# Two-layer attention kernel: the maxima of the second layer reduced one 512-column block at a time in a ring of three PSUM banks

## The chip, the cores and the metric

One core of a Trainium2 chip runs the whole program. The metric is the device time of one launch in microseconds; lower is better. One profiled execution of the kernel before was recorded, and all rows below come from it.

## The reference, cut to what matters

The input `x` has 4 batches of 1024 tokens and 128 features. A first attention layer with 8 heads of 64 is followed by a "graph" of six nodes, each a full attention over the tokens of its batch with 8 heads of 16. Only the graph is touched by the change.

```
for c in range(NUM_NOD):                       # 6 nodes
    q = ew[c, 0] * (nodes[in_q] @ We[eq] + be[eq])
    k = ew[c, 1] * (nodes[in_k] @ We[ek] + be[ek])
    v = ew[c, 2] * (nodes[in_v] @ We[ev] + be[ev])
    o = _mha(q, k, v, Wq[c], Wk[c], Wv[c], Wo[c])   # softmax over 1024 keys
    nodes[c] = act_w[c] * o + q
```

The softmax needs, for every query row and head, the maximum over the 1024 keys of the scores, before any exponential of that head can be taken.

## The kernel before

Six nodes times four batches make 24 **units**, and the graph works through them one after the other. Everything in a unit stands in a fixed order that Python loops write out for each engine; there is no scheduler. Engines meet through semaphores alone.

**Rounds.** TensorE (PE) walks through 74 rounds in a full unit. 64 of them are score rounds: two matmuls of 50x512 fill two banks of PSUM (`ps_max`, two buffers of 1024 columns used in turn), and ScalarE (ACT) takes the exponential of all 1024 columns in one instruction into `pt_b`. The other ten are listed in `PLAN`: round 2 and 50 turn maxima (`turn`, line 1563), 8 and 24 make the output of the unit before (`output`, lines 1611 and 1612), 11, 14, 17 and 20 project queries and keys of two units ahead (`project`, line 1524), 30 and 34 make values (`values`, line 1532). `bank_free` lets a round start only when the round two before it has been read out of the same `ps_max` buffer.

**Contexts.** After every second score round PE multiplies four exponentials with the values (`contexts`, line 1603, 4 matmuls that appear as 8 records, output `ps_ctx`). A unit has 32 such groups. This text calls the stretch from the start of one group to the start of the next a **step**, and names a step by the round that ends it: step 44 holds the group that begins after round 42, and rounds 43 and 44. Steps with nothing but score rounds and maxima are called plain; there are 22 in a unit (1, 6, 23, 28, 33, then every second number from 38 to 48 and from 53 to 73), and ten mixed ones: 4 and 51 with a turn, 9 and 26 with an output, 12, 15, 18 and 21 with a projection, 31 and 36 with values.

**Maxima.** While a unit runs, PE also makes the raw scores of the **next** unit, 128 blocks of 128 queries by 512 keys (48x512 matmuls, line 1556), only to find their row maxima. They go to three banks of PSUM: `ps_pair` (two banks) and `ps_misc` (one). VectorE (DVE) reduces what is there to maxima (`tensor_reduce`, line 1777). A piece is two blocks in `ps_pair` for even numbers and one block in `ps_misc` for odd numbers (`SIZES`), so there are 86 pieces. PE may fill a piece when DVE has reduced the piece two before it, the last user of the same banks:

```
if w > 1 or p >= 2:
    pe.wait_ge(mx_done, NM * (w - 1) + p - 1)
```

Heads lie in pairs on rows 0 to 47 and 64 to 111 of the array; two matmuls in a row on different halves overlap, and `in_turn` orders the two of a pair for that.

**The table.** `PIECE_SLOT` says where each piece stands. Slot 2r is just ahead of round r's own matmuls, slot 2r+1 just behind them and ahead of a context group. DVE takes the pieces in the same order. The table holds for units with all ten other rounds or as many rounds in all (the first 22); unit 22, with fewer rounds, spreads its pieces evenly, and the last unit has none.

Between pieces DVE takes four short reciprocals per unit, and at the end of each half of the pieces a small maximum over two chunks of keys (`mx_final`, line 1785), for which the turns wait.

Of the kernel before, what the change touches and what calls it, by code (L numbers as in the profile page):

```python
# [25 lines left out]
ALU = mybir.AluOpType  # L26
AX = mybir.AxisListType

P = 128
BATCH, TOK, DIM = 4, 1024, 128  # L30
HEADS, QUAD, DV = 8, 4, 16
SLOT = 32
CHUNK = 512
NCHUNK = TOK // CHUNK
KB = TOK // P
# [20 lines left out]
MROW_B = DV * len(TERMS)  # L56
# [13 lines left out]
BLOCKS = 2 * PIECES  # L70
# [1186 lines left out]
def graph(nc, psM, psP, psO, psX, sid, wpd, wvd, wfd, node, partd, invd, stored, units, x1d, ln_g, ln_b, out_rows):  # L1257
# [3 lines left out]
    with ExitStack() as ctx:  # L1261
# [71 lines left out]
        ROUND = [rounds_of(u) for u in range(UNITS)]  # L1333
        BASE = [sum(len(ROUND[w]) for w in range(u)) for u in range(UNITS + 1)]

        SIZES = []
        for q in range(2):
            while sum(SIZES) < BLOCKS * (q + 1):
                SIZES.append(min(2 - len(SIZES) % 2, BLOCKS * (q + 1) - sum(SIZES)))
        NM = len(SIZES)  # L1340
        HALF_M = NM // 2

        def exps(u, n):
            return NS // 2 * u + (n + 1) // 2
# [5 lines left out]
        def steps_at(u, r):  # L1350
# [4 lines left out]
        GROUP_ROUND = {BASE[u] + r: (S + 1) // KB - 1 for u in range(UNITS) for r in range(len(ROUND[u]))  # L1355
                       for S in steps_at(u, r) if S % KB == KB - 1}

        PIECE_SLOT = (2, 2, 4, 6, 9, 10, 12, 14, 16, 19, 19, 21, 24, 25, 26, 27, 29, 31, 32, 33, 35, 37,
# [3 lines left out]
        SLOTS_INNER = 2 * (NS // 2 + len(PLAN))  # L1362

        def pieces_at(u, r, half):
# [12 lines left out]
        with nc.Block() as block:  # L1377
# [141 lines left out]
            def _(pe):  # L1519
# [16 lines left out]
                last_rows = [None]  # L1536
# [9 lines left out]
                def maxima(w, p):  # L1546

                    if p % HALF_M == 0:
                        pe.wait_ge(stacked[p // HALF_M], STACK * (w + 1))
                    if w > 1 or p >= 2:  # L1550
                        pe.wait_ge(mx_done, NM * (w - 1) + p - 1)
                    at = sum(SIZES[:p])
                    for k in in_turn([(at + k) % 2 for k in range(SIZES[p])]):
                        pair, qb, kc, odd = (at + k) // (BLOCKS // 2), (at + k) // 4 % KB, (at + k) // 2 % 2, (at + k) % 2
                        rows = slice(P // 2 * odd, P // 2 * odd + MROW_B)
                        ins = pe.matmul((psP, psX)[p % 2][:, CHUNK * k:CHUNK * k + CHUNK],  # L1556
                                        qs[w % 2][rows, pair, P * qb:P * qb + P],
                                        ks[w % 2][rows, pair, CHUNK * kc:CHUNK * kc + CHUNK], start=True, stop=True)
                    ins.then_inc(mx_ready, 1)

                def turn_maxima(w, q, to):
                    pe.wait_ge(mx_final, 2 * w + q + 1)
# [210 lines left out]
            def _(dve):  # L1773
                def maxima(w, p):
                    dve.wait_ge(mx_ready, NM * (w - 1) + p + 1)
                    at, n = sum(SIZES[:p]), SIZES[p]
                    nc.vector.tensor_reduce(mx2[:, at:at + n], (psP, psX)[p % 2][:, 0:CHUNK * n].rearrange("p (h n) -> p h n", h=n),  # L1777
                                            AX.X, ALU.max).then_inc(mx_done, 1)
                    if p % HALF_M == HALF_M - 1:
                        q = p // HALF_M  # L1780
                        dve.wait_ge(mx_done, NM * (w - 1) + p + 1)
                        if w:
                            dve.wait_ge(mt_ready, 2 * (w - 1) + q + 1)
                        both = mx2[:, BLOCKS * q:BLOCKS * q + BLOCKS].rearrange("p (n k h) -> p n k h", k=2, h=2)
                        nc.vector.tensor_tensor(mx[:, PIECES * q:PIECES * q + PIECES].rearrange("p (h n) -> p n h", h=2),
                                                both[:, :, 0], both[:, :, 1], ALU.max).then_inc(mx_final, 1)
# [201 lines left out]
```

## Time and profile before

| | |
|---|---|
| time, median of 3 runs | 3016.4 us (3011.99 to 3019.83) |
| time of the profiled execution | 3020.31 us |
| its span, first to last instruction | 3018.5 us |
| busy share of the span | PE 95%, DVE 79%, ACT 72%, GpSimd 12% |
| mean granted clock of TensorE | 0.977 |

Busy time of PE is made of modelled ends of overlapping matmuls, so 95% doesn't say that the array is full. What a piece costs is read from the starts of instructions in the timeline: the start of the next one, less the start of this.

### The profile page before, as it was taken

Reading aid. Unit: us, or ns where it says so; the run is one execution under the profiler, and the core shown is the slowest. Engines: PE = TensorE matmul, PEld = TensorE weight load, DVE = VectorE, ACT = ScalarE, POOL = GpSimd, SP = SyncE. Lnnn points to the kernel's source line nnn. Section 1 sums busy time; section 2 is a strip of 40 time slices with the busy share of each in tenths; the row PEclk is TensorE's granted clock in tenths of the full one; section 3 lists DMA queues with packets and bytes.
Section 4 is the critical chain, followed back from the end, with each engine's and each line's share of the span. In section 5 each row is a group of like instructions: output and inputs, shape, how many; then the busy total and the mean of one; then the engine's idle time right before and its main releaser. Section 6 shows DMA issues by size and latency. Waiting matters only on the chain. (4 is left out here: it accounts for less than half of the span.)

```text
span 3018.5 us, 49064 instructions
## 1 busy us (share of the span) xinstructions
PE 2854.5 (95%) x18975; PEld 1291.1 (43%) x18975; DVE 2385.2 (79%) x3019; ACT 2159.6 (72%) x2738; POOL 353.0 (12%) x314
## 2 busy tenths in 40 slices
PE   6899999998699999999999999999999999999986
PEld 5556656654333333333333333333333333333332
DVE  7656566665778888888888888888888888888865
ACT  3556555555368888878787878787878788878776
POOL 0000000000001111111111111110111110111100
PEclk8999999999789999999999999999999999999998
DMA  7000000013423544453544453544454544444302
GB/s 160 25 9 16 16 12 12 5 62 72 93 60 97 114 80 98 88 116 96 117 78 100 88 114 100 113 78 103 93 107 102 111 77 105 95 102 105 66 21 67
DMA packets 146190, 239.49 MB, mean 79 GB/s; under 512 B 56802, under 2 KB 97142, under 8 KB 142630
## 3 DMA queue, kind: packets, MB, share of 16 engines
q1 hardware_dynamic: 145958, 236.36, 35.5%
q8 instruction: 150, 2.46, 0.4%
q14 instruction: 82, 0.67, 0.1%
HBM read 162.53 MB, written 70.98 MB: 77 GB/s over the span
## 5 line engine op out<-in xcount | busy, mean ns | idle before, releaser
L1749 ACT ACTIVATE pt_b<-ps_max 128x1024 f32<-128x1024 f32 x1516 | 1489.0, 1023 | 296.3 <-PE ps_max L1568 291.6
L1777 DVE TENSOR_REDUCE mx_b<-ps_pair 128x2 f32<-128x1024 f32 (+1 forms) x989 | 1191.5, 1205 | 110.5 <-PE ps_pair L1556 99.3
L1603 PE MATMUL ps_ctx<-pt_b,vs 128*32 128x512 f32 x6144 | 823.7, 608 | 1.8 <-ACT c_b L1732 1.8
L1777 DVE TENSOR_REDUCE mx_b<-ps_misc 128x1 f32<-128x512 f32 x989 | 676.4, 684 | 164.5 <-PE ps_misc L1556 160.8
L1568 PE MATMUL ps_max<-qs,ks 50*128 50x512 f32 x3032 | 766.4, 434 | 4.1 <-ACT pt_b L1749 0.6
L1556 PE MATMUL ps_pair<-ks,qs 48*128 48x512 f32 x1955 | 525.8, 464 | 24.3 <-DVE mx_b L1777 22.4
L1556 PE MATMUL ps_misc<-ks,qs 48*128 48x512 f32 x989 | 447.6, 453 | 12.1 <-DVE mx_b L1777 7.3
L1568 PEld LDWEIGHTS ps_max<-qs,ks 50*128 50x128 f32 x3032 | 346.6, 186 | 225.6 <-ACT pt_b L1749 137.6
L1556 PEld LDWEIGHTS ps_pair<-ks,qs 48*128 48x128 f32 x1955 | 202.7, 184 | 381.1 <-DVE mx_b L1777 350.9
L1556 PEld LDWEIGHTS ps_misc<-ks,qs 48*128 48x128 f32 x989 | 182.7, 185 | 380.5 <-DVE mx_b L1777 291.9
L931 ACT ACTIVATE pt<-ps_max,cb 128x512 f32<-128x512 f32 x340 | 214.6, 685 | 180.9 <-PE ps_max L658 117.6
L994 DVE TENSOR_REDUCE mx<-ps_max 128x2 f32<-128x1024 f32 x172 | 206.6, 1220 | 62.9 <-PE ps_max L629 39.2
L1603 PEld LDWEIGHTS ps_ctx<-pt_b,vs 128*32 128x32 f32 x6144 | 121.4, 108 | 239.3 <-issue 228.5
L651 PE MATMUL ps_max<-qs,ks 64*128 64x512 f32 x1020 | 162.9, 424 | 20.8 <-ACT pt L931 14.0
L931 ACT ACTIVATE pt<-ps_pair,cb 128x512 f32<-128x512 f32 x172 | 108.8, 684 | 93.9 <-PE ps_pair L658 53.8
L1928 POOL TENSOR_TENSOR part<-full,part 128x512 fp32r<-128x512 f32 x88 | 112.6, 1280 | 382.9 <-ACT part L1700 382.9
L1940 POOL TENSOR_TENSOR cn_b<-c_b,rec_b 128x512 f32<-128x512 f32 x48 | 62.0, 1292 | 702.1 <-DMA rec_b<-invd 668.5
L720 PE MATMUL ps_ctx<-pt,vs 128*32 128x512 f32 x1024 | 136.7, 607 | 0.6 <-ACT c_a L907 0.6
L651 PEld LDWEIGHTS ps_max<-qs,ks 64*128 64x128 f32 x1020 | 84.1, 186 | 114.2 <-issue 48.6
L994 DVE TENSOR_REDUCE mx<-ps_pair 128x2 f32<-128x1024 f32 x84 | 102.5, 1220 | 30.4 <-PE ps_pair L629 17.0
L1943 POOL TENSOR_TENSOR cn_b<-c_b,rec_b 128x512 f32<-128x512 f32 x47 | 60.3, 1284 | 415.1 <-DMA rec_b<-invd 401.0
L651 PE MATMUL ps_pair<-qs,ks 64*128 64x512 f32 x516 | 82.0, 423 | 9.1 <-ACT pt L931 6.9
(225 smaller groups left out, 2178.7 us busy)
## 6 DMA issues: line engine op xcount, KB each, us to landing
partd<-part SPq DMA_DIRECT2D x22, 2048.0 KB, 9.5
qs<-partd SPq DMA_DIRECT2D x288, 128.0 KB, 5.6
ks<-partd SPq DMA_DIRECT2D x288, 128.0 KB, 6.7
xv<-node SPq DMA_DIRECT2D x26, 512.0 KB, 5.5
xf<-node SPq DMA_DIRECT2D x24, 512.0 KB, 4.7
xq<-node SPq DMA_DIRECT2D x23, 512.0 KB, 3.8
xk<-node SPq DMA_DIRECT2D x23, 512.0 KB, 4.8
rec_b<-invd SPq DMA_DIRECT2D x368, 32.0 KB, 1.8
```

The costliest lines, as they stand in the source:

```text
L651: ins = pe.matmul(to[:, CHUNK * odd:CHUNK * odd + CHUNK], minus[rows] if a is None else a[q][rows, j, keys], b[q][rows, j, queries], start ...
L720: ins = pe.matmul(psO[SLOT * i:SLOT * i + SLOT, :], vs[q][:, kb, i], pt[:, s % 2, i], start=kb == 0, stop=kb == KB - 1)
L931: ins = act.activation(pt[:, s % 2, 2 * j + odd], slot("score", hh, n)[:, CHUNK * odd:CHUNK * odd + CHUNK], ACT.Exp, scale=SCALE_A, bias=c ...
L994: nc.vector.tensor_reduce(out, slot("maxima", hh, p)[:].rearrange("p (k n) -> p k n", k=2), AX.X, ALU.max).then_inc(mx_done, 1)
L1556: ins = pe.matmul((psP, psX)[p % 2][:, CHUNK * k:CHUNK * k + CHUNK], qs[w % 2][rows, pair, P * qb:P * qb + P], ks[w % 2][rows, pair, CHUNK ...
L1568: return pe.matmul(to[:, CHUNK * (n % 2):CHUNK * (n % 2) + CHUNK], ks[u % 2][rows, h // 2, P * kb:P * kb + P], qs[u % 2][rows, h // 2, CHU ...
L1603: ins = pe.matmul(psO[SLOT * i:SLOT * i + SLOT, :], vs[u % 2][:, kb, QUAD * (s // HALF_STEPS) + i], pt[:, (QUAD * S + i) % ENTRIES], start ...
L1749: act.activation(pt[:, e:e + 2].rearrange("p k n -> p (k n)"), at[:], ACT.Exp, scale=SCALE_B).then_inc(exp_done, 1)
L1777: nc.vector.tensor_reduce(mx2[:, at:at + n], (psP, psX)[p % 2][:, 0:CHUNK * n].rearrange("p (h n) -> p h n", h=n), AX.X, ALU.max).then_inc ...
L1928: nc.gpsimd.tensor_tensor(part[:, qk, 1, cols], full[:, qk, cols], part[:, qk, 0, cols].bitcast(F32), ALU.subtract).then_inc(split_done, 1)
L1940: nc.gpsimd.tensor_tensor(cn[:, 0, c], c32[:, c], rec[0][:], ALU.mult).then_inc(cn_done, 1)
L1943: nc.gpsimd.tensor_tensor(cn[:, 1, c], c32[:, c], rec[1][:], ALU.mult).then_inc(cn_alone, 1)
```

## The change

The maxima of the graph's units are made and reduced one block a piece: 128 pieces of 512 columns instead of 86 of 1024 and 512. The three banks become a ring of single banks, in the order first half of `ps_pair`, `ps_misc`, second half of `ps_pair`. PE may fill a piece when the piece three before it has been reduced. The table has 128 entries from slot 0 to 147.

```
-        SIZES = []
-        for q in range(2):
-            while sum(SIZES) < BLOCKS * (q + 1):
-                SIZES.append(min(2 - len(SIZES) % 2, BLOCKS * (q + 1) - sum(SIZES)))
-        NM = len(SIZES)
-        HALF_M = NM // 2
+        NM = 2 * BLOCKS
+        HALF_M = BLOCKS
+        MAX_SLOTS = (psP[:, 0:CHUNK], psX[:], psP[:, CHUNK:TOK])
+
+        def max_slot(w, p):
+            return MAX_SLOTS[(NM * (w - 1) + p) % 3]
...
-        PIECE_SLOT = (2, 2, 4, 6, 9, 10, 12, 14, 16, 19, 19, 21, 24, 25, 26, 27, 29, 31, 32, 33, 35, 37,
+        PIECE_SLOT = (0, 1, 3, 4, 6, 6, 8, 9, 10, 12, 12, 14, 16, 16, 17, 17, 19, 20, 21, 21, 23, 25,
...
-                    if w > 1 or p >= 2:
-                        pe.wait_ge(mx_done, NM * (w - 1) + p - 1)
-                    at = sum(SIZES[:p])
-                    for k in in_turn([(at + k) % 2 for k in range(SIZES[p])]):
-                        pair, qb, kc, odd = (at + k) // (BLOCKS // 2), (at + k) // 4 % KB, (at + k) // 2 % 2, (at + k) % 2
-                        rows = slice(P // 2 * odd, P // 2 * odd + MROW_B)
-                        ins = pe.matmul((psP, psX)[p % 2][:, CHUNK * k:CHUNK * k + CHUNK],
-                                        qs[w % 2][rows, pair, P * qb:P * qb + P],
-                                        ks[w % 2][rows, pair, CHUNK * kc:CHUNK * kc + CHUNK], start=True, stop=True)
-                    ins.then_inc(mx_ready, 1)
+                    if w > 1 or p >= 3:
+                        pe.wait_ge(mx_done, NM * (w - 1) + p - 2)
+                    pair, qb, kc, odd = p // (BLOCKS // 2), p // 4 % KB, p // 2 % 2, p % 2
+                    rows = slice(P // 2 * odd, P // 2 * odd + MROW_B)
+                    last_rows[0] = odd
+                    pe.matmul(max_slot(w, p), qs[w % 2][rows, pair, P * qb:P * qb + P],
+                              ks[w % 2][rows, pair, CHUNK * kc:CHUNK * kc + CHUNK], start=True, stop=True).then_inc(mx_ready, 1)
...
-                    at, n = sum(SIZES[:p]), SIZES[p]
-                    nc.vector.tensor_reduce(mx2[:, at:at + n], (psP, psX)[p % 2][:, 0:CHUNK * n].rearrange("p (h n) -> p h n", h=n),
-                                            AX.X, ALU.max).then_inc(mx_done, 1)
+                    nc.vector.tensor_reduce(mx2[:, p:p + 1], max_slot(w, p), AX.X, ALU.max).then_inc(mx_done, 1)
```

How PE's rows stand in three steps of a full unit follows; `ps_pair` and `ps_misc` are maxima (x2 is two blocks), `ps_max<-qs,ks` are scores, `ps_ctx` the context group that begins a step and the one that begins the next. Line numbers of the changed kernel differ by a few.

Step 42, plain. Before:

```order
L1603 MATMUL ps_ctx<-pt_b,vs 32x512 x4
L1568 MATMUL ps_max<-qs,ks 128x512 x2
L1556 MATMUL ps_misc<-ks,qs 128x512
L1556 MATMUL ps_pair<-ks,qs 128x512 x2
L1568 MATMUL ps_max<-qs,ks 128x512 x2
L1603 MATMUL ps_ctx<-pt_b,vs 32x512 x4
```

Now:

```order
L1602 MATMUL ps_ctx<-pt_b,vs 32x512 x4
L1557 MATMUL ps_misc<-ks,qs 128x512
L1557 MATMUL ps_pair<-ks,qs 128x512
L1567 MATMUL ps_max<-qs,ks 128x512 x2
L1557 MATMUL ps_pair<-ks,qs 128x512
L1567 MATMUL ps_max<-qs,ks 128x512 x2
L1557 MATMUL ps_misc<-ks,qs 128x512
L1602 MATMUL ps_ctx<-pt_b,vs 32x512 x4
```

The step held three blocks between its two score rounds; it now holds four, two at its beginning, one in the middle and one at its end.

Step 26, with the output of the unit before (`xf,wf` and `cn_b,wf`). Before:

```order
L1603 MATMUL ps_ctx<-pt_b,vs 32x512 x4
L1556 MATMUL ps_pair<-ks,qs 128x512 x2
L1611 MATMUL ps_max<-xf,wf 128x512
L1612 MATMUL ps_max<-cn_b,wf 128x512
L1556 MATMUL ps_misc<-ks,qs 128x512
L1556 MATMUL ps_pair<-ks,qs 128x512 x2
L1568 MATMUL ps_max<-qs,ks 128x512 x4
L1556 MATMUL ps_misc<-ks,qs 128x512
L1603 MATMUL ps_ctx<-pt_b,vs 32x512 x4
```

Now:

```order
L1602 MATMUL ps_ctx<-pt_b,vs 32x512 x4
L1557 MATMUL ps_pair<-ks,qs 128x512
L1557 MATMUL ps_misc<-ks,qs 128x512
L1610 MATMUL ps_max<-xf,wf 128x512
L1611 MATMUL ps_max<-cn_b,wf 128x512
L1557 MATMUL ps_pair<-ks,qs 128x512 x2
L1567 MATMUL ps_max<-qs,ks 128x512 x2
L1557 MATMUL ps_misc<-ks,qs 128x512
L1567 MATMUL ps_max<-qs,ks 128x512 x2
L1602 MATMUL ps_ctx<-pt_b,vs 32x512 x4
```

Six blocks have become five: behind the output stood four, the last of them just ahead of the contexts, and now stand three.

Step 36, with values (`wv_b,xv`). Before:

```order
L1603 MATMUL ps_ctx<-pt_b,vs 32x512 x4
L1556 MATMUL ps_pair<-ks,qs 128x512 x2
L1532 MATMUL ps_max<-wv_b,xv 128x128 x4
L1556 MATMUL ps_misc<-ks,qs 128x512
L1556 MATMUL ps_pair<-ks,qs 128x512
L1568 MATMUL ps_max<-qs,ks 128x512 x2
L1556 MATMUL ps_misc<-ks,qs 128x512
L1568 MATMUL ps_max<-qs,ks 128x512 x2
L1556 MATMUL ps_pair<-ks,qs 128x512 x2
L1603 MATMUL ps_ctx<-pt_b,vs 32x512 x4
```

Now:

```order
L1602 MATMUL ps_ctx<-pt_b,vs 32x512 x4
L1557 MATMUL ps_misc<-ks,qs 128x512
L1557 MATMUL ps_pair<-ks,qs 128x512
L1534 MATMUL ps_max<-wv_b,xv 128x128 x4
L1557 MATMUL ps_pair<-ks,qs 128x512
L1557 MATMUL ps_misc<-ks,qs 128x512
L1567 MATMUL ps_max<-qs,ks 128x512 x2
L1557 MATMUL ps_pair<-ks,qs 128x512
L1567 MATMUL ps_max<-qs,ks 128x512 x2
L1557 MATMUL ps_pair<-ks,qs 128x512
L1602 MATMUL ps_ctx<-pt_b,vs 32x512 x4
```

Of the seven blocks six are left; the last place held a piece of two and holds one block.

Over a unit of the table, the blocks per step were and are:

| steps | blocks before | blocks now |
|---|---|---|
| plain: 55, 71 | 4 each | 4 each |
| plain: 59 | 5 | 4 |
| plain: 42, 44, 61, 73 | 3 each | 4 each |
| plain: 33 | 3 | 2 |
| the other 14 plain | 3 each | 3 each |
| turn: 4, 51 | 5, 6 | 5, 6 |
| output: 9, 26 | 6, 6 | 6, 5 |
| projection: 12, 15, 18, 21 | 4, 6, 6, 6 | 5, 6, 6, 5 |
| values: 31, 36 | 6, 7 | 6, 6 |

## Rows read from the trace of the kernel before

**Rows 1.** The page, busy time of each engine over the span.

```profile
PE 2854.5 (95%) x18975; PEld 1291.1 (43%) x18975; DVE 2385.2 (79%) x3019; ACT 2159.6 (72%) x2738; POOL 353.0 (12%) x314
```

**Rows 2.** One line's instructions: turns, with count, first and last start.

```profile
L1563 PE MATMUL ps_max<-ident_sb,mx_b x43: 283/284/287, 926.6 to 2822.1; 128*32 128x128 f32 x43
```

**Rows 3.** Windows: one unit: length, busy PE, PEld, DVE, ACT, POOL, clock, DMA.

```profile
1466.53:1556.66 90.13, 88.78 (x549) 34.84 (x547) 78.62 (x93) 72.63 (x87) 13.67 (x13) 1.00 0.47 99
```

**Rows 4.** Groups on DVE in that unit: busy us, mean ns, idle before.

```profile
L1777 DVE TENSOR_REDUCE mx_b<-ps_pair 128x2 f32<-128x1024 f32 x43 | 52.3, 1217 | 4.6 <-PE ps_pair L1556 4.1
L1777 DVE TENSOR_REDUCE mx_b<-ps_misc 128x1 f32<-128x512 f32 x43 | 29.4, 684 | 7.1 <-PE ps_misc L1556 7.0
```

**Rows 5.** Timeline of a plain step with three blocks: start, length, instruction.

```profile
1520.71 1.07 PE L1603 MATMUL ps_ctx<-pt_b,vs 128*32 128x512 f32 x8
...
1522.84 1.07 PE L1603 MATMUL ps_ctx<-pt_b,vs 128*32 128x512 f32 x8
```

**Rows 6.** Timeline of a plain step with four blocks.

```profile
1530.92 1.06 PE L1603 MATMUL ps_ctx<-pt_b,vs 128*32 128x512 f32 x8
1531.91 0.50 PE L1556 MATMUL ps_misc<-ks,qs 48*128 48x512 f32 x1
...
1532.45 0.69 DVE L1777 TENSOR_REDUCE mx_b<-ps_misc 128x1 f32<-128x512 f32 x1 [0.29 <-PE ps_misc L1556]
...
1533.20 0.50 PE L1556 MATMUL ps_misc<-ks,qs 48*128 48x512 f32 x1
1533.63 0.64 PE L1603 MATMUL ps_ctx<-pt_b,vs 128*32 128x512 f32 x4
```

**Rows 7.** Timeline of a plain step with five blocks.

```profile
1535.77 1.07 PE L1603 MATMUL ps_ctx<-pt_b,vs 128*32 128x512 f32 x8
...
1537.31 1.22 DVE L1777 TENSOR_REDUCE mx_b<-ps_pair 128x2 f32<-128x1024 f32 x1 [0.32 <-PE ps_pair L1556]
...
1538.59 0.50 PE L1556 MATMUL ps_pair<-ks,qs 48*128 48x512 f32 x2 [0.63 <-DVE mx_b L1777]
1539.02 0.64 PE L1603 MATMUL ps_ctx<-pt_b,vs 128*32 128x512 f32 x4
```

**Rows 8.** Timeline of step 26, with the output.

```profile
1494.14 1.06 PE L1603 MATMUL ps_ctx<-pt_b,vs 128*32 128x512 f32 x8
...
1497.48 0.49 PE L1556 MATMUL ps_misc<-ks,qs 48*128 48x512 f32 x1
...
1497.59 0.69 ACT L1726 ACTIVATE nt_b<-ps_max,wf 128x512 f32<-128x512 f32 x1 [1.60 <-PE ps_max L1612]
...
1498.76 0.50 PE L1556 MATMUL ps_misc<-ks,qs 48*128 48x512 f32 x1
1499.19 0.64 PE L1603 MATMUL ps_ctx<-pt_b,vs 128*32 128x512 f32 x4
```

**Rows 9.** Timeline of step 36, with values.

```profile
1507.33 1.06 PE L1603 MATMUL ps_ctx<-pt_b,vs 128*32 128x512 f32 x8
...
1510.38 0.69 DVE L1777 TENSOR_REDUCE mx_b<-ps_misc 128x1 f32<-128x512 f32 x1 [0.29 <-PE ps_misc L1556]
...
1510.99 0.68 DVE L1777 TENSOR_REDUCE mx_b<-ps_pair 128x1 f32<-128x512 f32 x1
...
1511.73 0.50 PE L1556 MATMUL ps_pair<-ks,qs 48*128 48x512 f32 x2
...
1512.16 1.06 PE L1603 MATMUL ps_ctx<-pt_b,vs 128*32 128x512 f32 x8
```

**Rows 10.** Timeline: behind a projection, pair, scores, single, then contexts.

```profile
1483.26 0.50 PE L1556 MATMUL ps_pair<-ks,qs 48*128 48x512 f32 x2
1483.60 0.40 PE L1568 MATMUL ps_max<-qs,ks 50*128 50x512 f32 x2
1483.84 0.40 PE L1556 MATMUL ps_misc<-ks,qs 48*128 48x512 f32 x1
1484.16 0.64 PE L1603 MATMUL ps_ctx<-pt_b,vs 128*32 128x512 f32 x4
```

8 rows, old and new, of the table PIECE_SLOT are left out of this document.

## The prediction, made before the changed kernel was run

> **What bounds the kernel now.** I read the page first: over the span PE is busy 95%, DVE 79%, ACT 72% [rows 1]. PE's figure is made of modelled ends, so it says where to look and not how full PE is. Then one line's instructions: 43 turns, two a unit, from 926.6 to 2822.1 us, which makes 21 units of (2822.1 - 926.6) / 21 = 90.26 us each [rows 2]. The kernel is thus a period repeated some 22 times, and the change is worth 22 times what it does to one. In the windows the unit from 1466.53 to 1556.66 is 90.13 us long at full clock (1.00, the level of 2.4 GHz), DVE busy 78.62 us of it and ACT 72.63 [rows 3]. No engine but PE is near its end on the average, so the unit's length is PE's own work plus what PE stands still for. The grouping of DVE shows where the slack lies: 4.6 us and 7.1 us of idle time, all of it waiting for blocks that PE had not yet made [rows 4]. PE and DVE wait for each other in turn, and the timeline of single steps tells how.
>
> A context group holds PE 0.99 us (1530.92 to 1531.91) [rows 6]. A plain step with three blocks is 1522.84 - 1520.71 = 2.13 us [rows 5]. With four blocks it is 1533.63 - 1530.92 = 2.71 [rows 6], with five 1539.02 - 1535.77 = 3.25 [rows 7]. Counting step by step in the whole stretch from 1466 us on, and in unit 22 at the end, whose steps stand in another order, the same lengths come back: 2.12 to 2.20 for three blocks, 2.69 to 2.71 for four (eight steps, of which one stands in the rows), 3.25 to 3.26 for five (six steps). So a block beyond three costs (3.25 - 2.13) / 2 = 0.56 us, though two matmuls on different halves together take only 1483.84 - 1483.60 = 0.24 us [rows 10]. The extra is a wait, and rows 6 show its links. The first block of the step starts at 1531.91, DVE starts on it 0.54 us later (1532.45), runs 0.69, and 0.06 us after its end (1533.14) the fourth block starts, at 1533.20, in the same bank; contexts follow 0.43 us behind. The fourth block can't come sooner than 1.29 us after the first, and a step that begins and ends with a block, four in all, is 0.99 + 1.29 + 0.43 = 2.71 us. With a piece of two in the last place it waits for the first pair: 1537.31 + 1.22 + 0.06 = 1538.59, as the row has it, and the step is 3.25 [rows 7].
>
> **The change, part by part.** *The ring.* Before, a pair waits for the pair two pieces back and a single for the single two back: always the same bank, which means three blocks back. Now it is written as three pieces back, and it is three blocks back again. What falls away is that a block waits for its neighbour in a pair: the pair's banks come free at start + 1.28, a single's at start + 0.75, both from the rows above. Only where a pair was waited for does this help: step 59 and step 36. A four-block step already waits for a single, and the chain of 1.29 us stands in it unchanged.
>
> *DVE's work.* Next to each other on DVE, a single starts 0.61 us after a single (1510.38 to 1510.99) [rows 9], although each is 0.69 long. A pair is 1217 ns against 684 for a single [rows 4]; with the same overlap of 0.08 it holds DVE 1.14. A unit costs 43 x (1.14 + 0.61) = 75.3 us before and 128 x 0.61 = 78.1 now: 2.8 us more of DVE in a unit in which it idles 11.7 [rows 4]. In a three-block step it has 2.13 - 3 x 0.61 = 0.30 us left. So this part costs nothing as long as that cover holds; without it, 2.8 us a unit. The Trainium skill (Perfetto Trace Analysis, section Optimizing Scalar/DVE Operations) speaks against the change here: it gives DVE some 125 ns of overhead for each instruction on PSUM and advises to group when the engine is saturated. By that figure 42 more instructions would be an estimated 5.3 us; the trace's pitch says 2.8.
>
> *The table.* This is the larger part, since a block's price depends on the step it falls in. Over the 22 plain steps, the excess over three blocks was 1 + 1 + 2 = 4 and is now seven steps with one each: 3 x 0.565 = **+1.70 us** a unit. Step 33 drops to two blocks, an even run of six matmuls that begins and ends two by two; 0.12 less, between 0 and 0.24: **-0.12**.
>
> Step 26 is 1499.19 - 1494.14 = 5.05 us, its last block at 1498.76 waiting for the first behind the output (1497.48 + 1.28) [rows 8]. With that block gone the next lock is ACT: it copies the output until 1497.59 + 0.69 = 1498.28, which is 0.80 us after the output's end, and the last two scores go into that buffer. They start at about 1498.35 and contexts 0.38 behind, 1498.73 instead of 1499.19: **-0.45**.
>
> Step 36 is 1512.16 - 1507.33 = 4.83 [rows 9]. Its last pair waited until 1511.73 at the end of a chain of two reductions. The first block behind the values stood at 1510.38 - 0.54 = 1509.84, 2.51 us into the step. Now the last block waits for this one, so the step is 2.51 + 1.29 + 0.43 = 4.23: **-0.60**.
>
> Step 21 loses one block of six. Matmuls on the two halves go by pairs: 0.34, 0.24, and 0.32 for a last single, 0.90 for five [rows 10]; a run of four is between 0.58 and 0.90. I take **-0.27**. Step 12 gains a block by the same rule at 0 to 0.23; I take 0, since it makes a run of three into one of four. In steps 4 and 51 the last block now waits for a single that stands a reduction later in DVE's queue: about **+0.16** in all, at most 0.4.
>
> The sum is 1.70 - 0.12 - 0.45 - 0.60 - 0.27 + 0.16 = +0.42 us a unit. In the steps with a projection, third and fifth blocks come to their bank within 0.1 us of its release (the third of a chain is free at 0.53 + 2 x 0.61 + 0.75 = 2.50 us after the first started, PE wants it at 2.5). For these I add 0.15, between 0 and 0.5. Then 22 x (0.42 + 0.15) = **+12.5 us**. Made against the profiled execution, 3020.31, that is 3033; its own time stands 3.9 us above the median of the runs shown, so for a median I say 3016.4 + 12.5 = **3029**. Unit 22 keeps its excess (16 blocks beyond three in its plain steps before and now), and the last unit has no pieces. What is queued behind a waiting block on PE is the score, and behind that ACT; ACT idles 17 us of the unit [rows 3] and follows PE's step.
>
> **The rivals.** *The finer ring frees PE (faster).* The fourth block of a step finds its bank free, because DVE begins on single blocks as they come. Were a four-block step to cost as little as one of three, seven steps would save 7 x 0.565 = 3.95 us and the unit be 0.57 - 3.95 = -3.4 us, 2942 us in all. The Trainium skill (Perfetto Trace Analysis, section Optimizing Scalar/DVE Operations) has a sentence for this side: if Scalar or Vector aren't saturated but cause bubbles on other engines, breaking up instructions may let work complete sooner. Against it stands that the waited-for block is already a single in rows 6 and the link is no shorter. A half of it, by waits in the mixed steps that go fully (0.3 each in ten steps, 3 us a unit), gives 0.57 - 3 = -2.4 us and 2963. It decides by one number: with seven four-block steps, each 0.08 us cheaper, the sum is zero, which is a first-to-fourth distance of 1.2 us instead of 1.29. I give the faster side 0.24, most of it near 3000, where the mixed steps gain more than I took.
>
> *DVE becomes the bound (slower).* If single reductions followed at 0.68 instead of 0.61, DVE would need 128 x 0.68 = 87 us and two for the rest in a unit of 90; the chains of three in the six projection and value steps come 0.14 late each, some 0.8 us, and the four-block steps find DVE still busy at their first block. I price it at 1.5 us a unit more: 3029 + 33 = 3062. The pitch of rows 9 speaks against it; 0.12.
>
> *Nothing is left of it.* The table's loss and the mixed steps' gain cancel to 0.2 us a unit: 3012 to 3021. Both are near 2 us, so an error of a fifth does it; 0.24.
>
> **How the numbers follow.** My forecast, 3020 to 3042 by the bounds of its terms (0.2 to 1.2 us a unit), has 0.4. A measurement of this kernel can tell about 0.3%, 9 us, from no change; part of the forecast lies inside. Slower by over 0.3%: most of my own case and the DVE case, 0.46; within: 0.30; faster: 0.24. The range must hold eight in ten: up to the middle of the DVE case, 3055, and down into the faster one, 2988.
>
> **What would show it.** In the profile after: a unit of 90.7 us between turns; plain four-block steps at 2.7 us with a first-to-fourth start distance of 1.29; DVE busy 80 to 84 us of it, with singles 0.61 apart where they queue; steps 26 and 36 near 4.6 and 4.2. I am wrong if four-block steps are short, if singles stand further apart than 0.61, or if two blocks in neighbouring banks disturb each other.

## The result, and the profile after

The changed kernel takes 3034.4 us in the median of 4 runs (3032.61 to 3036.22); the kernel before took 3015.5 beside it. The ratio is 1.0058, interval 1.0039 to 1.0077: slower by 11.8 to 23 us. Below, the medians of two experiments leave out one slow execution each (3447 and 3761 us, at granted clocks of 0.74 and 0.66). The profiled execution took 3035.97 us with a span of 3034.1. First the page of the changed kernel, busy time over the span:

```profile
PE 2891.3 (95%) x18975; PEld 1297.1 (43%) x18975; DVE 2446.9 (81%) x3985; ACT 2171.3 (72%) x2738; POOL 352.8 (12%) x314
```

These are to be held against [rows 1]: DVE has 966 instructions and 61.7 us more, PE as many matmuls as before and 36.8 us more of modelled time. A matmul that is issued less tightly counts as longer, so this figure can't say where PE stood still. The turns give the period, as in [rows 2] (one line's instructions, with first and last start):

```profile
L1562 PE MATMUL ps_max<-ident_sb,mx_b x43: 284/285/285, 930.5 to 2836.7; 128*32 128x128 f32 x43
```

That is (2836.7 - 930.5) / 21 = 90.77 us a unit against 90.26, 10.7 us over 21 units. Of the 15.6 us between the two spans, 3.9 lie ahead of the first of these turns (930.5 against 926.6) and 1.0 behind the last. The windows of one unit in the middle of the graph (length, busy PE, PEld, DVE, ACT, POOL, clock, DMA):

```profile
1473.70:1564.37 90.67, 89.86 (x547) 34.79 (x547) 81.58 (x135) 73.09 (x87) 13.61 (x13) 1.00 0.47 99
```

Against [rows 3] the unit is 0.54 us longer at the same clock (medians over all units: 90.74 and 90.15), and DVE works 2.96 us more in it. The groups of DVE in that unit (busy us, mean ns, idle before):

```profile
L1775 DVE TENSOR_REDUCE mx_b<-ps_pair 128x1 f32<-128x512 f32 x86 | 56.2, 682 | 5.2 <-PE ps_pair L1557 4.5 <-PE ps_misc L1557 0.2
L1775 DVE TENSOR_REDUCE mx_b<-ps_misc 128x1 f32<-128x512 f32 x42 | 28.6, 681 | 3.8 <-PE ps_pair L1557 2.2 <-PE ps_misc L1557 1.3
L1782 DVE TENSOR_TENSOR mx_b<-mx_b 128x32 f32<-128x32 f32 x3 | 2.1, 706 | 0.1
```

DVE still waits for PE for 9.0 us, where it waited 11.7 [rows 4]. The third row is the small maximum over two chunks of keys; its three instructions in this stretch take 706 ns in the mean.

Step 44, one of the four that grew from three blocks to four, in the timeline (start, length, instruction):

```profile
1525.08 1.06 PE L1602 MATMUL ps_ctx<-pt_b,vs 128*32 128x512 f32 x8
1526.08 0.50 PE L1557 MATMUL ps_misc<-ks,qs 48*128 48x512 f32 x1
...
1526.61 0.69 DVE L1775 TENSOR_REDUCE mx_b<-ps_misc 128x1 f32<-128x512 f32 x1 [0.23 <-PE ps_misc L1557]
...
1527.36 0.50 PE L1557 MATMUL ps_misc<-ks,qs 48*128 48x512 f32 x1
1527.78 0.64 PE L1602 MATMUL ps_ctx<-pt_b,vs 128*32 128x512 f32 x4
```

The chain of [rows 6] is unchanged: the first block at 1526.08, its reduction from 1526.61 to 1527.30, the fourth block in the same bank 0.06 later, 1.28 us after the first, contexts 0.42 behind. The step is 2.70. Step 36 ends now as follows, to be held against [rows 9]:

```profile
1513.89 1.06 PE L1602 MATMUL ps_ctx<-pt_b,vs 128*32 128x512 f32 x8
...
1515.42 0.69 DVE L1775 TENSOR_REDUCE mx_b<-ps_pair 128x1 f32<-128x512 f32 x1 [0.37 <-PE ps_pair L1557]
1516.03 0.68 DVE L1775 TENSOR_REDUCE mx_b<-ps_misc 128x1 f32<-128x512 f32 x1
1516.40 0.49 PE L1557 MATMUL ps_pair<-ks,qs 48*128 48x512 f32 x2
...
1517.68 0.50 PE L1557 MATMUL ps_pair<-ks,qs 48*128 48x512 f32 x1
1518.11 0.64 PE L1602 MATMUL ps_ctx<-pt_b,vs 128*32 128x512 f32 x4
```

The first block behind the values starts 2.51 us into the step, the last one 1.28 later, and the step is 4.22. Singles on DVE stand 0.61 apart (1515.42, 1516.03).

Read off in this way, from one context group to the next, the steps compare so (us). Each column shows the same unit, the eighth, of its kernel; four kernels of the experiments below stand beside the two, and "last version" is the one with two blocks moved. The 9 steps left out, of three or six blocks, are within 0.05 us of before in all of these. The last row is the median length of a unit over the whole graph.

| step | before | after | ring, old places | old pairs, new places | three-block table | last version |
|---|---|---|---|---|---|---|
| 4 | 3.26 | 3.57 | 3.30 | 3.47 | 3.34 | 3.34 |
| 12 | 3.63 | 3.71 | 3.63 | 3.67 | 4.00 | 4.00 |
| 15, 18 | 3.90, 3.89 | 3.89, 3.91 | 3.95, 3.96 | 3.85, 4.14 | 3.90, 3.97 | 3.92, 3.95 |
| 21, 23 | 3.91, 2.18 | 3.60, 2.13 | 3.98, 2.24 | 4.08, 2.14 | 4.13, 2.13 | 3.61, 2.12 |
| 26 | 5.05 | 4.61 | 5.05 | 4.63 | 4.96 | 4.63 |
| 33 | 2.12 | 1.90 | 2.13 | 1.90 | 2.12 | 2.12 |
| 36 | 4.83 | 4.22 | 4.81 | 5.07 | 4.42 | 4.22 |
| 38, 40 | 2.13, 2.17 | 2.13, 2.13 | 2.12, 2.25 | 2.12, 2.13 | 2.25, 2.13 | 2.12, 2.14 |
| 42, 44 | 2.13, 2.12 | 2.71, 2.70 | 2.13, 2.14 | 2.71, 2.13 | 2.25, 2.14 | 2.23, 2.69 |
| 46, 51 | 2.13, 3.84 | 2.12, 3.90 | 2.13, 3.89 | 2.19, 4.12 | 2.41, 3.91 | 2.15, 3.91 |
| 55, 71 | 2.71, 2.70 | 2.71, 2.71 | 2.71, 2.72 | 3.25, 3.25 | 2.71, 2.70 | 2.71, 2.70 |
| 59, 61 | 3.25, 2.12 | 2.71, 2.71 | 3.29, 2.12 | 2.70, 2.14 | 2.70, 2.14 | 2.70, 2.12 |
| 63, 67 | 2.13, 2.18 | 2.11, 2.14 | 2.12, 2.23 | 2.36, 2.17 | 2.35, 2.13 | 2.36, 2.15 |
| 73, 1 | 2.12, 2.14 | 2.71, 2.13 | 2.12, 2.13 | 2.69, 2.14 | 2.14, 2.35 | 2.70, 2.13 |
| unit, median | 90.15 | 90.74 | 90.61 | 92.58 | 90.80 | 90.30 |

### The profile page after: what moved, and what is told of

It is laid out like the page before. It is cut to its first block and busy times, and to the rows that moved or that the text cites. A ratio compares the mean times of both kernels' runs of the same rounds, so it can differ in the third digit from the quotient of the medians.

```text
span 3034.1 us, 50030 instructions
## 1 busy us (share of the span) xinstructions
PE 2891.3 (95%) x18975; PEld 1297.1 (43%) x18975; DVE 2446.9 (81%) x3985; ACT 2171.3 (72%) x2738; POOL 352.8 (12%) x314
## 5 line engine op out<-in xcount | busy, mean ns | idle before, releaser
L1748 ACT ACTIVATE pt_b<-ps_max 128x1024 f32<-128x1024 f32 x1516 | 1490.3, 1024 | 314.0 <-PE ps_max L1567 303.9
L1775 DVE TENSOR_REDUCE mx_b<-ps_pair 128x1 f32<-128x512 f32 x1963 | 1283.8, 682 | 150.1 <-PE ps_pair L1557 109.2
L1567 PE MATMUL ps_max<-qs,ks 50*128 50x512 f32 x3032 | 822.1, 435 | 0.7 <-ACT pt_b L1748 0.7
L1557 PE MATMUL ps_pair<-ks,qs 48*128 48x512 f32 x1963 | 773.0, 449 | 21.1 <-PEq L360 7.8
L1775 DVE TENSOR_REDUCE mx_b<-ps_misc 128x1 f32<-128x512 f32 x981 | 668.5, 681 | 76.2 <-PE ps_misc L1557 39.2
L1557 PEld LDWEIGHTS ps_pair<-ks,qs 48*128 48x128 f32 x1963 | 330.2, 186 | 546.3 <-DVE mx_b L1775 491.8
L1567 PEld LDWEIGHTS ps_max<-qs,ks 50*128 50x128 f32 x3032 | 376.0, 186 | 190.7 <-ACT pt_b L1748 140.8
L1557 PE MATMUL ps_misc<-ks,qs 48*128 48x512 f32 x981 | 439.5, 448 | 6.7 <-DVE mx_b L1775 2.8
```

What stands on the lines that cost most here:

```text
L1557: pe.matmul(max_slot(w, p), qs[w % 2][rows, pair, P * qb:P * qb + P], ks[w % 2][rows, pair, CHUNK * kc:CHUNK * kc + CHUNK], start=True, st ...
L1567: return pe.matmul(to[:, CHUNK * (n % 2):CHUNK * (n % 2) + CHUNK], ks[u % 2][rows, h // 2, P * kb:P * kb + P], qs[u % 2][rows, h // 2, CHU ...
L1748: act.activation(pt[:, e:e + 2].rearrange("p k n -> p (k n)"), at[:], ACT.Exp, scale=SCALE_B).then_inc(exp_done, 1)
L1775: nc.vector.tensor_reduce(mx2[:, p:p + 1], max_slot(w, p), AX.X, ALU.max).then_inc(mx_done, 1)
```

## The experiments

In all of them only the graph's maxima, their table or the exponentials are edited. Diffs are against the changed kernel unless said otherwise. Ratios are to the kernel before, run beside them.

**The two halves of the change, each alone.** The ring with every block in the slot where its piece stood before, so that each old slot stands once for every block of its piece (first line of the table):

```
-        PIECE_SLOT = (0, 1, 3, 4, 6, 6, 8, 9, 10, 12, 12, 14, 16, 16, 17, 17, 19, 20, 21, 21, 23, 25,
+        PIECE_SLOT = (2, 2, 2, 4, 4, 6, 9, 9, 10, 12, 12, 14, 16, 16, 19, 19, 19, 21, 24, 24, 25, 26,
```

> The ring of three single banks with the old places: each old piece of two blocks becomes two pieces of one in the same slot, so every step holds the blocks that it held before. My theory (a step's length comes from how many blocks it holds, since the fourth block waits 1.29 us from the first, and the ring's wait is still three blocks back): nearly the time of before, 3015 to 3021 us; step 59 with five blocks 3.25 to 3.32 us, step 26 about 5.05, step 36 about 4.83. Rival 1 (42 more VectorE instructions a unit make the loss): the loss of the changed kernel is there with any table, 3030 to 3040. Rival 2 (the finer ring itself gains and the new table loses more): under 3005.

Measured: 3031.45 us, ratio 1.0043 (1.003 to 1.0056), unit 90.61. The expectation (3015 to 3021) was missed: the ring by itself costs 0.46 us a unit. Its timeline, in step 15:

```profile
1483.49 1.06 PE L1602 MATMUL ps_ctx<-pt_b,vs 128*32 128x512 f32 x8
...
1484.33 0.68 DVE L1775 TENSOR_REDUCE mx_b<-ps_misc 128x1 f32<-128x512 f32 x1
...
1484.82 0.40 PE L1567 MATMUL ps_max<-qs,ks 50*128 50x512 f32 x2
1485.02 1.29 DVE L1775 TENSOR_REDUCE mx_b<-ps_pair 128x1 f32<-128x512 f32 x2
1485.06 0.50 PE L1557 MATMUL ps_misc<-ks,qs 48*128 48x512 f32 x1
```

The same place in the kernel before:

```profile
1480.26 1.06 PE L1603 MATMUL ps_ctx<-pt_b,vs 128*32 128x512 f32 x8
...
1481.04 0.68 DVE L1777 TENSOR_REDUCE mx_b<-ps_misc 128x1 f32<-128x512 f32 x1
...
1481.59 0.40 PE L1568 MATMUL ps_max<-qs,ks 50*128 50x512 f32 x2
1481.79 1.22 DVE L1777 TENSOR_REDUCE mx_b<-ps_pair 128x2 f32<-128x1024 f32 x1
1481.83 0.45 PE L1556 MATMUL ps_misc<-ks,qs 48*128 48x512 f32 x1
```

In both, the third block of the step starts 1.57 us into it. Before, the reduction that it waits for had ended at 1481.04 + 0.68 = 1481.72, 0.11 ahead. In the ring it ends at 1484.33 + 0.68 = 1485.01, and the block starts 0.05 behind that, the distance seen wherever a block waits; the projection then follows 0.43 behind it, where it followed 0.38 behind before. The third block has lost its margin, because DVE is held longer ahead of it: a record of two singles is 1.29 long where the pair's is 1.22. One such place seems to cost 0.05 to 0.08 (steps 15, 18, 21, 23, 40, 51, 67), 4 and 59 pay 0.04 each.

**The pairs of before, in the slots of the new table.** Each piece stands where the new table has its last block (first line, against the kernel before):

```
-        PIECE_SLOT = (2, 2, 4, 6, 9, 10, 12, 14, 16, 19, 19, 21, 24, 25, 26, 27, 29, 31, 32, 33, 35, 37,
+        PIECE_SLOT = (1, 3, 6, 6, 9, 10, 12, 14, 16, 17, 19, 20, 21, 23, 26, 28, 29, 31, 32, 32, 35, 37,
```

> The kernel before, pieces of two and one, with a table of 86 places that puts each piece where its last block stands in the new table; the counts of blocks per step come near the new ones (seven blocks beyond three in the plain steps, where four were). My theory: plain steps add 3 x 0.565 us a unit; where a single now waits for a single behind a pair (step 36: MM m V MM ss m ss m) the wait grows to about 2.4 us, so step 36 is near 5.6 us; steps 4 and 51 0.3 and 0.4 us more, steps 26 and 33 less by 0.45 and 0.22. In all 2.5 us a unit, 3071 us, slower than the changed kernel, since a pair's banks come free later than a single's. Rival (the table costs the same whatever the ring is): 3027.

Measured: 3087.2 us, ratio 1.0241 (1.0224 to 1.0257), unit 92.58. In the unit this is the size expected, 2.4 us against 2.5. The median of the times is 16 us above the 3071 expected, but it goes with the clock: the four executions took 3075.36, 3084.26, 3090.16 and 3095.61 us at mean granted clocks of 0.977, 0.974, 0.971 and 0.967, and the executions of before beside it had 0.975 to 0.980. PE's groups in its unit (busy us, mean ns, idle before) show the pair's wait:

```profile
L1556 PE MATMUL ps_pair<-ks,qs 48*128 48x512 f32 x85 | 21.9, 458 | 2.8 <-DVE mx_b L1777 2.8
```

What follows from the two: +0.46 for the ring in the old places, +2.4 for the new places with the old pairs, and +0.59 for both together. The new places only work with single blocks, and with them cost 0.13 more than the old ones; the times, 1.0058 and 1.0043 with intervals that overlap, don't show so small a difference. The two halves of the change can't be added. "New places with old pairs" isn't quite the new table, since a pair brings its first block along: steps 55 and 71 hold five blocks in it instead of four, step 36 seven instead of six, 44 and 61 three instead of four, and 33 one instead of two.

**Whose wait is the fourth block's?** Each reduction reads only the first 256 of its 512 columns, so that the maxima leave half the keys out; the exponentials' input is scaled by 1e-4 beside it, for values that stay finite. PE, ACT and the number of instructions stay as they are.

```
-  nc.vector.tensor_reduce(mx2[:, p:p + 1], max_slot(w, p), AX.X, ALU.max)
+  nc.vector.tensor_reduce(mx2[:, p:p + 1], max_slot(w, p)[:, 0:CHUNK // 2], AX.X, ALU.max)
```

> The changed kernel, but each reduction reads only 256 of its 512 columns, so half of the keys are left out of the maxima, and the exponentials are taken of scores scaled by 1e-4 so that they stay finite; all matmuls, waits and counts are as in the changed kernel. A reduction shortens by 256 columns, about 0.27 us. My theory (the fourth block waits for the first one's reduction): first-to-fourth distance 1.02 instead of 1.29, a plain four-block step 2.44 instead of 2.71, three-block steps 2.13 as before; with steps 4, 36 and 51 about 2.9 us a unit, 2967 us. Rival 1 (TensorE's own work sets the four-block step): no change, 3034. Rival 2 (VectorE's total work is the bound): a gain of far more than 3 us a unit, three-block steps shorten too.

Measured: 2958.3 us, ratio 0.9803 (0.9788 to 0.9818), a unit in the middle 87.55 (median over all 87.74). A four-block step in its timeline:

```profile
1491.66 1.06 PE L1602 MATMUL ps_ctx<-pt_b,vs 128*32 128x512 f32 x8
...
1492.66 0.50 PE L1557 MATMUL ps_pair<-ks,qs 48*128 48x512 f32 x1
...
1493.19 0.42 DVE L1775 TENSOR_REDUCE mx_b<-ps_pair 128x1 f32<-128x256 f32 x1 [0.69 <-PE ps_pair L1557]
...
1493.67 0.50 PE L1557 MATMUL ps_pair<-ks,qs 48*128 48x512 f32 x1
1494.10 0.64 PE L1602 MATMUL ps_ctx<-pt_b,vs 128*32 128x512 f32 x4
```

The reduction is 0.27 shorter, the fourth block comes 1.01 us after the first instead of 1.28, and the step falls from 2.70 to 2.44. Steps with three blocks stay at 2.12 to 2.14. DVE is busy 48.5 of the 87.55 us: 33 us of its work are gone, and the unit is only 3 shorter. So the fourth block waits for the latency of one reduction and not for DVE's throughput, and a three-block step of 2.13 doesn't wait for DVE. That it doesn't wait for ScalarE either is shown by the shorter exponentials below, which leave it at 2.12 to 2.14.

**Fewer four-block steps.** A table with four blocks in three plain steps, 55, 59 and 71, and three in the others: one block each goes from 42, 44, 61 and 73 to 12, 21, 26 and 33, and one inside step 36 stands elsewhere. One line of it:

```
-                      77, 79, 81, 81, 82, 82, 83, 85, 86, 87, 88, 89, 91, 92, 93, 94, 95, 97, 98, 99, 100, 100,
+                      70, 71, 75, 75, 77, 79, 81, 81, 82, 83, 83, 86, 87, 88, 91, 92, 93, 94, 95, 97, 98, 99,
```

> The changed kernel with another table: steps 42, 44, 61 and 73 get three blocks again, the four blocks go to steps 12, 21, 26 and 33, and step 36 has three blocks ahead of the values and three behind them. My theory: four plain steps go from 2.71 to 2.13 us (-2.3 a unit), step 36 from 4.22 to about 3.95 (-0.25), the four that receive a block grow by 0.19, 0.30, 0.24 and 0.23 us (+0.96): -1.6 us a unit, 2999 us, faster than both kernels. Rival 1 (VectorE is the bound, its 128 reductions are the same): 3034, no change. Rival 2 (only the mean number of blocks matters, the queue evens out): within 5 us of 3034.

Measured: 3033.5 us, ratio 1.0048 (1.0036 to 1.006), unit 90.80. A clear miss: 1.6 us a unit less was expected, and it got none. By the step table the four steps saved 2.16 us, and step 4 another 0.23. Two things ate that: steps 12 (0.29), 21 (0.53), 26 (0.35), 33 (0.22) and 36 (0.20) grew by 1.6 us in all, and steps 38, 42, 46, 63 and 1 came out at 2.25 to 2.41 instead of 2.13. Step 36 was expected to shrink by 0.25, and step 21 to grow by 0.30 only; what these two wait for stays open. Step 46 in its timeline:

```profile
1515.64 2.90 ACT L1748 ACTIVATE pt_b<-ps_max 128x1024 f32<-128x1024 f32 x3
...
1515.92 1.07 PE L1602 MATMUL ps_ctx<-pt_b,vs 128*32 128x512 f32 x8
...
1516.91 0.50 PE L1567 MATMUL ps_max<-qs,ks 50*128 50x512 f32 x2
1517.25 0.40 PE L1557 MATMUL ps_misc<-ks,qs 48*128 48x512 f32 x1
1517.25 0.40 PE L1557 MATMUL ps_pair<-ks,qs 48*128 48x512 f32 x1
1517.66 0.50 PE L1567 MATMUL ps_max<-qs,ks 50*128 50x512 f32 x2
1518.00 0.40 PE L1557 MATMUL ps_pair<-ks,qs 48*128 48x512 f32 x1
1518.33 0.64 PE L1602 MATMUL ps_ctx<-pt_b,vs 128*32 128x512 f32 x4
```

Here ScalarE runs three exponentials back to back, the second of which ends at 1515.64 + 2 x 0.97 = 1517.58; the scores at 1517.66 go into the buffer that it frees. A copy of the contexts (0.60 us) had held ScalarE just before. So far this is argued from one place; the next pair of runs tested it.

**Shorter exponentials, with both tables.** In every unit but the first each exponential takes 832 of its 1024 columns, so the rest of the exponentials isn't computed:

```
+  cols = 2 * CHUNK if u == 0 else 832
-  act.activation(pt[:, e:e + 2].rearrange("p k n -> p (k n)"), at[:], ACT.Exp,
+  act.activation(pt[:, e:e + 2].rearrange("p k n -> p (k n)")[:, 0:cols], at[:, 0:cols], ACT.Exp,
```

> The table of the run 'three', and from unit 1 on each exponential takes 832 of its 1024 columns, so a part of the exponentials is left out and ScalarE has 0.16 us less in each of its 64 instructions. In 'three' the scores of steps 38, 42, 46, 63 and 1 waited for ScalarE (2.25 to 2.41 us where 2.13 is the length of three blocks). My theory (ScalarE, late after steps of three blocks in a row, took back what the table saved): these five steps fall to 2.13, 1.0 us a unit less, about 3011 us; steps 12, 21, 26 and 36 stay as in 'three', since VectorE sets them. Rival (those steps are long for another reason, matmuls on the same half in a row): no change, 3033.

> The changed kernel with the same shorter exponentials. My theory: its four-block steps already give ScalarE time, no plain step waits for it, so the unit shortens by less than 0.2 us; 3029 to 3034. Rival (ScalarE is in the bound of the changed kernel as well): 1 us a unit less, 3012 or under.

Measured with the three-block table: 3015.0 us, ratio 0.9967 (0.994 to 0.9995), unit 89.88 where it was 90.80, and steps 38, 46, 63 and 1 fell to 2.12, step 42 stayed at 2.24. With the table of the change: 3031.0, ratio 1.0026 (1.0008 to 1.0044), unit 90.67 against 90.74. So ScalarE isn't what holds the changed kernel, and it takes back a part where three-block steps stand in a row. Step 42 waits for something else. In the trace of the first of the two runs its third block starts at 1515.56, 0.05 behind the end of the reduction that frees its bank (two reductions from 1514.23, 1.28 long together), which is the distance of a block that waits; in step 44, of 2.12, that bank had long been free. This points to DVE, and no run tested it.

**Reductions shortened by 32 columns, ring with old places.** 480 of 512 columns a block (the maxima leave 32 keys a block out, and the exponentials' input is scaled as above), which takes some 0.03 us from each reduction:

```
-  nc.vector.tensor_reduce(mx2[:, p:p + 1], max_slot(w, p), AX.X, ALU.max)
+  nc.vector.tensor_reduce(mx2[:, p:p + 1], max_slot(w, p)[:, 0:480], AX.X, ALU.max)
```

> The ring with the old places, where each reduction reads 480 of 512 columns (32 keys left out of the maxima, exponentials of scores scaled by 1e-4 to stay finite). Two reductions of 480 hold VectorE as long as one of 1024, about 1.14 us. My theory (the ring cost 0.48 us a unit because two single reductions hold VectorE 1.21 us instead of 1.14, and that shows where a block comes to its bank just as it is freed): steps 15, 18 and 21 back from 3.95 to 3.90, steps 23, 40 and 67 back near 2.18, unit 90.0 to 90.1 us, 3015 to 3020 us. Rival (the cost is in the semaphores or in the matmuls of the ring): steps stay at 3.95 and the unit at 90.5.

Measured: 3005.7 us, ratio 0.9931 (0.9906 to 0.9956), unit 89.61, 1.0 us less than with 512 columns and more than expected. Steps 15 and 18 fall to 3.86 and 3.85, 23 and 40 to 2.13 and 2.14. So these steps hang on a few hundredths of a microsecond of DVE and not on the semaphores or matmuls of the ring, as the rival had it. They end below the 3.90 and 2.18 of the kernel before, and four- and five-block steps gained as well (2.67, 3.24), which I had left out: shorter reductions would presumably help the old pairs too, and no run tried that.

**The small maximum, taken later.** In the changed kernel it stands in step 1, right behind the last reduction, while GpSimd adds (`cn_b<-cn_b`). This part of the changed kernel's timeline:

```profile
1472.47 1.28 POOL L1942 TENSOR_TENSOR cn_b<-cn_b 128x512 f32<-128x512 f32 x1
...
1472.91 0.91 DVE L1782 TENSOR_TENSOR mx_b<-mx_b 128x32 f32<-128x32 f32 x1
...
1473.70 1.06 PE L1602 MATMUL ps_ctx<-pt_b,vs 128*32 128x512 f32 x8
1473.72 1.28 DVE L1775 TENSOR_REDUCE mx_b<-ps_pair 128x1 f32<-128x512 f32 x2
```

and the same instruction in the kernel before, begun ahead of GpSimd's addition:

```profile
1555.80 0.21 DVE L1785 TENSOR_TENSOR mx_b<-mx_b 128x32 f32<-128x32 f32 x1
...
1555.98 1.28 POOL L1945 TENSOR_TENSOR cn_b<-cn_b 128x512 f32<-128x512 f32 x1
```

The small maximum ends 0.07 us behind GpSimd's instruction (1472.91 + 0.91 = 1473.82 against 1473.75) when that one began first. It is 0.91 long where 0.21 is enough, and the reductions behind it come late for step 4. It takes 0.76 to 0.99 us in 20 of the first 22 units; before, the places missed each other more often, and it took 0.66 to 1.11 in 6 of 23. The Trainium skill (SBUF — State Buffer, section Who interferes with whom) says that a DVE instruction with two SBUF inputs contends with a GpSimd instruction that reads SBUF, and that the order of issue decides which of the two is blocked. The trace agrees for the case in which GpSimd is first, by the 0.91 us. Moved two pieces down, out of that instruction's time:

```
+                    if p == HALF_M - 1:
+                        chunks(w, 0)
+                    elif p == 1 and w > 1:
+                        chunks(w - 1, 1)
+                    elif p == NM - 1 and w == LAST:
+                        chunks(w, 1)
```

> The changed kernel, with the small maximum over two chunks of keys of the second half taken by VectorE two pieces later. In the changed kernel it takes 0.76 to 0.99 us instead of 0.22 in 20 of 22 units, ending with an addition of GpSimd. My theory (it waits for GpSimd's instruction, and the reductions behind it make step 4 longer, 3.57 where I had put 3.4): it takes 0.22 us, step 4 falls to 3.35 to 3.4, 0.2 us a unit, 3030 us. Rival (it is long because of the new layout of its inputs): it stays at 0.9 wherever it stands, and no time changes.

Measured: 3032.4 us, ratio 1.0034 (1.0016 to 1.0053), unit 90.58 against 90.74, step 4 at 3.35 instead of 3.57. The gain is read from the unit; the interval of the times overlaps with that of the changed kernel. The instruction is 0.20 again in most units, and still 0.58 to 1.09 in 4 of 22:

```profile
1468.39 1.29 POOL L1948 TENSOR_TENSOR cn_b<-cn_b 128x512 f32<-128x512 f32 x1
...
1470.22 0.20 DVE L1778 TENSOR_TENSOR mx_b<-mx_b 128x32 f32<-128x32 f32 x1
```

**One and two blocks moved.** On top of the later maximum, the first version takes a block from step 42 to step 33; the second also one from step 61 to step 12:

```
 step 42: slots 82, 82, 83, 85  ->  82, 83, 83         step 33: slot 65  ->  65, 65
 step 61: slots 120, 120, 122, 123  ->  120, 121, 122  step 12: slot 25  ->  25, 25
```

> The ring with the later small maximum (unit 90.58 us in its run) and one block moved: step 42 gets three blocks instead of four, step 33 three instead of two. Theory (a plain step's fourth block costs 0.57, and ScalarE takes over only where three-block steps stand in a row): step 42 falls from 2.71 to 2.13 to 2.25, step 33 rises from 1.90 to 2.12, unit about 90.2 to 90.3 us, the level of the kernel before (90.15), total within 0.3% of before. Rival (every wait taken out of a plain step comes back in ScalarE's exponentials): unit stays at 90.5 to 90.6 and the total 0.3 to 0.5% above before.

> The same with one more block moved: step 61 gets three blocks instead of four and the first projection step, 12, six instead of five. Theory: step 61 falls from 2.71 to 2.13, step 12 rises from 3.71 to 4.00 as in the run with three blocks in nearly all plain steps, unit about 89.9 to 90.0 us, 0.3 less than with one block moved, total 0.1 to 0.4% below before. Rival (the saved wait is given back by ScalarE in steps 61 to 67): unit as with one block moved or above, 90.2 to 90.5.

Measured: 3023.3 us, ratio 1.001 (0.9994 to 1.0026), unit 90.30, and 3023.1 us, ratio 1.0017 (1.0 to 1.0033), unit 90.30. The first came out as the theory has it: 42 at 2.23, 33 at 2.13. Of the second the rival's forecast held: step 61 fell to 2.12, step 12 paid 0.29, and step 63 rose to 2.36. The windows of a unit of it:

```profile
1462.72:1552.94 90.22, 89.53 (x548) 34.68 (x547) 81.16 (x135) 72.72 (x87) 13.64 (x13) 1.00 0.46 99
```

and step 63 in its timeline:

```profile
1536.33 2.91 ACT L1748 ACTIVATE pt_b<-ps_max 128x1024 f32<-128x1024 f32 x3
...
1538.32 0.50 PE L1567 MATMUL ps_max<-qs,ks 50*128 50x512 f32 x2
```

The scores at 1538.32 go when the second exponential is done (1536.33 + 2 x 0.97 = 1538.27), as in step 46 of the three-block table. No version with all the work in it beat the kernel before.

## Why the prediction came true, step by step

The forecast was +0.57 us a unit and +12.5 us in all; measured were +0.54 in the unit compared, +0.59 between medians, and +18.9 in the times.

**The chain of 1.29 us** held in every kernel with full reductions (1.28 in the row above), and half reductions moved it by just what the shorter reduction saves. The four-block and five-block steps, forecast at +1.70, measured +1.80 (42, 44, 61 and 73 together +2.34, 59 -0.54).

**The mixed steps** (us, measured, with the forecast behind it): 26 -0.44 (forecast -0.45), 36 -0.61 (-0.60), 21 -0.31 (-0.27), 33, a plain one, -0.22 (-0.12: two blocks save nearly all that the even run could give), 12 +0.08 (0). Steps 4 and 51 were mis-sized: +0.37 instead of +0.16. Of this, 0.22 is the small maximum that waits for GpSimd, which the prediction had not among its terms; with it out of the way the two come to +0.15. The allowance of +0.15 for tight places wasn't needed: the twenty steps left are 0.1 shorter together.

**The ring "costs nothing" while DVE's cover holds**: wrong as an effect by itself. The prediction gave nothing to the ring, 0.42 us a unit to the places and 0.15 to tight places; measured one by one, with the ring first, it is 0.46 for the ring and 0.13 for the places, and with the places first 2.4 for the places and -1.8 for the ring. DVE had the 11.7 us of idle time that I pointed to, and the ring with the old places still costs 0.46 a unit, because the cover has to be there at the block that is waited for and not in the sum. Nor did the ring alone help steps 59 and 36, where the prediction said that it would: they stay at 3.29 and 4.81, for the last of two blocks waits for the last of two reductions. Step 59 is shortened by the table, which has one block less there: with the old pairs in the new places it is 2.70 too. Step 36 needed both, 5.07 with the old pairs in the new places and 4.22 with singles. That the sum came out all the same is because I read each step with both edits in it.

**What was luck.** The terms are off by +0.10 (plain steps with four or five blocks), +0.21 (4 and 51) and +0.08 (12) on one side, and by -0.10 (33), -0.04 (21) and -0.28 (the tight places) on the other. They cancel to the 0.03 us a unit between +0.57 and +0.54. The mechanism of the four-block step, the largest term, was right; that the whole fits to 0.03 isn't owed to it.

**The rivals.** The finer ring doesn't free PE: the distance from the first to the fourth block is 1.28, above the 1.2 from which that rival would decide. DVE as the bound: singles stand 0.61 apart, DVE is busy 81.6 of 90.7 us, in the range given, and with 33 us less of its work the unit fell by 3 only. The cancellation missed by the 0.5 us a unit that the plain steps' seven excesses leave.

**The rest, 18.9 against 22 x 0.59 = 13.0.** The interval of the result, 11.8 to 23 us, takes in 13.0, and the clock accounts for much of the difference. 58 executions of the kernel before, run beside the experiments, had mean granted clocks of 0.971 to 0.984. A straight line through their times gives 3020.0 us at 0.977 and 2.1 us less for each 0.001 more, with 1.5 us of scatter. (A 59th, at 0.930, took 3047.48 us and lies far from the line, so this holds for the narrow band alone.) The four executions of the changed kernel had 0.975 to 0.977; carried along that line to 0.977 they are at 3032.3 us in the mean, an estimated 12.3 more than before, which is the 22 units. The same estimate gives 56 us for the old pairs in the new places, where 55 had been expected. Whether the change itself lowers the mean clock isn't shown.

In the profiled pair 3.9 us lie ahead of the first turn (930.5 against 926.6). Windows at the start of the graph, the kernel before:

```profile
830.00:860.00 30.00, 27.44 (x104) 8.57 (x101) 16.21 (x18) 14.63 (x18) 3.83 (x3) 0.68 0.00 1
860.00:895.00 35.00, 34.17 (x227) 14.40 (x226) 30.50 (x36) 28.66 (x34) 2.57 (x2) 1.00 0.31 96
```

and after:

```profile
830.00:860.00 30.00, 29.92 (x91) 10.27 (x90) 14.85 (x25) 13.60 (x17) 2.54 (x2) 0.51 0.01 2
860.00:895.00 35.00, 34.13 (x215) 13.87 (x219) 29.97 (x51) 27.93 (x33) 3.83 (x3) 1.00 0.23 84
```

The graph begins at a granted clock of 0.50 (1.2 GHz; from 830 to 840 us in both kernels) and is at 1.00 from 860 us on. In between the changed kernel stays at 0.50 until 855, with PE busy all the time, while before it is at 0.66 to 0.77 from 840 to 855. But it isn't a matter of the two kernels: the same stretch has 0.72, 0.94, 0.85, 0.79 and 0.77 in runs of the ring with old places, the three-block table, half reductions, the later maximum and the last version. Whether the change moves that moment on the average, or this profile caught a late one, the runs don't settle.

## What to carry to other kernels

Where two engines pass a few buffers back and forth, count the blocks between two fixed points of the bound engine and compare them with the number of buffers: the block that needs the first one's bank again can't start sooner than the latency of fill and reduction behind it (1.28 us here), however idle the other engine is on the average. Here that makes a step 0.58 us longer (2.71 against 2.13), more than a block's own work. A finer ring takes nothing from that latency; it only allows other places, so ring and table have to be judged together, step by step. And a saved wait is worth its price only up to the next engine's pace and to what the moved block costs elsewhere: of 2.16 us saved in four steps, ScalarE's two exponentials, 1.94 us of a 2.13 us step, took back 0.92, and the steps that took the blocks 1.6.

## What the runs showed of the hardware that was not expected

- A DVE maximum of 128x32 from two SBUF operands takes 0.20 to 0.22 us by itself and 0.91 when a GpSimd addition of 128x512 (1.28 us) began 0.44 us ahead of it: it ends 0.07 us behind that one.
- Two reductions of 512 columns next to each other stand 0.61 apart and hold DVE 1.28 to 1.29 us together, one of 1024 columns 1.21 to 1.22. In the ring with the old places, blocks without a margin and 0.4% of the time go with that 0.07, and 32 columns less in each reduction gave back more than that.
- 256 columns less in a reduction make it 0.27 us shorter (0.69 to 0.42), about a column a nanosecond.
- Executions of one kernel differ by their mean granted clock: 3075.36 us at 0.977 and 3095.61 at 0.967 for the old pairs in the new places, some 2 us for each 0.001.
